# A two-layer graph network on one core: ranking the batch two further on in pieces between VectorE's wide steps

## What is computed

```python
h = jnp.maximum(_layernorm(x, axis=-1), 0.0)
x = x + segment_sum((h * node_vec1)[src], dst, 12500) * node_vec1_n2      # layer 0
h = jnp.maximum(_layernorm(x, axis=-1), 0.0)
x = x + (1.0 + eps[0]) * h + segment_sum(relu(h[src] + edge_attr), dst, 12500)   # layer 1
```

## Time and profile before

| | |
|---|---|
| median of 3 runs | 4801.34 us (4799.08 to 4803.71) |
| the profiled execution, its own time | 4791.23 us |
| span of the profiled execution | 4789.2 us |
| granted TensorE clock, mean | 0.914 |
| layer 0, from one batch's first dst_rel to the next | 113.5 to 122.7 us |

### The profile page before, as it was taken

One profiled execution on the slowest core, in us unless ns is written; L12 is line 12 of the kernel. 1 busy time (PEld: TensorE's weight loads), 2 busy tenths in 40 slices (PEclk: granted clock), 3 DMA queues, 4 the chain that ended last, 5 costly groups with the idle time before them and its releaser, 6 DMA issues.

```text
span 4789.2 us, 130194 instructions
## 1 busy us (share of the span) xinstructions
PE 3721.2 (78%) x43852; PEld 2888.9 (60%) x43852; DVE 3812.7 (80%) x11454; ACT 3261.3 (68%) x9090; POOL 3497.5 (73%) x3590
## 2 busy tenths in 40 slices
PE   0388888888888888888888899467767777777775
PEld 0266666666666666666666666356666666666664
DVE  9788888888888888888888886767777776777775
ACT  1377777777777777777777777456666766666664
POOL 6757777777777777777777777477777777777774
PEclk9999999999999999999999999778888888888887
DMA  6322222222222222222222221211212221211221
GB/s 111 63 51 54 57 54 54 54 56 54 54 54 56 54 53 54 56 54 53 54 56 54 53 54 44 72 39 54 57 43 54 57 57 54 58 49 48 57 57 26
DMA packets 439702, 262.77 MB, mean 55 GB/s; under 512 B 334660, under 2 KB 423732, under 8 KB 432632
## 3 DMA queue, kind: packets, MB, share of 16 engines
q1 hardware_dynamic: 322488, 187.55, 16.7%
q0 software_dynamic: 110816, 60.69, 6.7%
q10 hardware_dynamic: 5728, 5.82, 0.5%
HBM read 172.96 MB, written 80.85 MB: 53 GB/s over the span
## 4 chain that ended last, share of the span: by engine, by line
PE 32%; POOL 23%; DVE 19%; issue 13%; ACT 10%; DMA 2%; DVEq 1%; ACTq 0%; SPq 0%; POOLq 0%
POOL stage L759 22%; PE candidates L1247 18%; PE plain_ps L1259 7%; DVE arena L1753 7%; ACT message L987 5%; DVE arena L1729 4%; ACT centered L956 2%; PE sorted_agg L1187 2%; PE candidates L1157 1%; ACT arena L880 1%; POOL message L759 1%; PE key_rows L1230 1%; DMA stage<-in_edge_attr 1%; DVE counts L1475 1%; PE key_rows L1139 1%
## 5 line engine op out<-in xcount | busy, mean ns | idle before, releaser
L771 POOL DMA_INDIRECT records<-stage,place_i x1875 | 1879.0, 1002 | 696.2 <-issue 652.0
L759 POOL DMA_INDIRECT stage<-table,src_plain x1250 | 1246.9, 997 | 409.1 <-issue 377.3
L987 ACT ACTIVATE message<-candidates,member_is 128x96 bf16<-128x96 f32 x4560 | 1170.7, 377 | 429.4 <-PE candidates L1247 426.3
L1753 DVE TENSOR_SCALAR arena<-window_iota,dst_rel 128x224 bf16<-128x224 f16 (+1 forms) x4800 | 1091.2, 302 | 37.8
L880 ACT ACTIVATE arena<-key_rows 125x640 f16<-125x640 f16 x1000 | 653.2, 716 | 215.1 <-DVE arena L1729 83.2
L1187 PE MATMUL sorted_agg<-arena 128*96 128x224 bf16 (+1 forms) x5000 | 654.1, 285 | 161.0 <-DVE arena L1753 109.6
L1259 PE MATMUL plain_ps<-summed,message 128*96 128x224 bf16 x4560 | 609.2, 269 | 68.2 <-ACT message L987 68.2
L1187 PEld LDWEIGHTS sorted_agg<-arena 128*96 128x96 bf16 x5000 | 543.7, 137 | 186.1 <-issue 118.6
L1259 PEld LDWEIGHTS plain_ps<-summed,message 128*96 128x96 bf16 x4560 | 490.7, 128 | 269.6 <-ACT message L987 127.4
L1729 DVE TENSOR_SCALAR arena<-arena,row_key 125x1280 bf16<-125x1280 f16 x1000 | 554.7, 555 | 96.5 <-ACT arena L880 64.6
L1139 PE MATMUL key_rows<-ident,record 128*125 128x128 f16 x5000 | 425.8, 235 | 239.2 <-DMA record<-records 96.2
(11 more groups left out here) (228 smaller groups left out, 5139.0 us busy)
## 6 DMA issues: line engine op xcount, KB each, us to landing
record<-records SPq DMA_DIRECT2D x50, 1650.0 KB
stage<-in_edge_attr SPq DMA_DIRECT2D x125, 400.0 KB, 3.2
records<-pad SPq DMA_DIRECT2D x25, 1650.0 KB, 11.9
records<-stage,place_i POOLq DMA_INDIRECT x1875
stage<-table,src_plain POOLq DMA_INDIRECT x1250
message<-table,mid_src POOLq DMA_INDIRECT x288
xs<-in_x SPq DMA_DIRECT2D x8, 390.6 KB
table<-parts ACTq DMA_DIRECT2D x4, 585.9 KB
```

The costliest lines, as they stand in the source:

```text
L759: pool.indirect_dma_start(message[:, k, j, :] if l == 0 else rows[:, k, j, :], None, table0 if l == 0 else table1, bass.IndirectOffsetOnAx ...
L771: pool.indirect_dma_start(records, bass.IndirectOffsetOnAxis(ap=place_i[:, h, e:e + 1], axis=0), stage[:, h, e, :], None).then_inc(scatter ...
L987: last = nc.scalar.activation(direct_message[n % DB][:, m * WIDE:(m + 1) * WIDE], candidates[n % 2][:, m * WIDE:(m + 1) * WIDE], ACT.Copy, ...
L1753: last = nc.vector.tensor_scalar(dst_onehot(g, t), window_iota[:, 0:WA if tile == 0 else WT], dst_rel[:, h, tile:tile + 1], None, ALU.is_e ...
```

## The change

`rank_within` is cut in two functions, `rank_buckets` (the small operations and the comparisons) and `rank_scans` (the three scans of one unit). DVE now makes the buckets and the first unit's scans behind wide step 2, the second unit's scans behind wide step 3 and the third's behind wide step 4. `rank_sums` and `rank_places` move from behind the last wide step to behind wide step 6, so that wide step 7 comes after them. PE's `prefixes` move from ahead of wide step 6 to ahead of wide step 5. Operations, shapes and semaphores are the same.

```diff
@@ TensorE, step0
-                            if n == FIRST[SUBS - 2] and left_after(b) >= 2:
+                            if n == FIRST[SUBS - 3] and left_after(b) >= 2:
                                 prefixes(b + 2)
@@ VectorE
             def rank_within(b, h, u):
+                rank_buckets(b, h, u)
+                for v in range(SORTED):
+                    rank_scans(b, v)
+
+            def rank_buckets(b, h, u):
                 nth = [0]
...
-                for v in range(SORTED):
-                    for some in SCANS:
-                        last = nc.vector.tensor_tensor_scan(counts[:, v, some], goes_on[:, 0:some.stop - some.start],
-                                                            in_bucket[:, v, some], 0.0, ALU.mult, ALU.add)
-                        if v < SORTED - 1 or some != SCANS[-1]:
-                            step(last)
-                last.then_inc(scans_ready, 1)
-                assert nth[0] == RANK1
+                assert nth[0] == 8 + SORTED
+
+            def rank_scans(b, v):
+                nth = [8 + SORTED + v * len(SCANS)]
...
+                for some in SCANS:
+                    last = nc.vector.tensor_tensor_scan(counts[:, v, some], goes_on[:, 0:some.stop - some.start],
+                                                        in_bucket[:, v, some], 0.0, ALU.mult, ALU.add)
+                    if v < SORTED - 1 or some != SCANS[-1]:
+                        step(last)
+                if v == SORTED - 1:
+                    last.then_inc(scans_ready, 1)
+                    assert nth[0] == RANK1
@@ VectorE, step0
                             sort_some(b, q, i, s)
                             direct_onehots(b, h, s)
-                            if s == SUBS - 3 and more:
-                                rank_within(b + 2, h, u + 1)
-                        if more:
-                            rank_sums(b + 2)
-                            rank_places(b + 2, h, u + 1)
+                            if s == 2 and more:
+                                rank_buckets(b + 2, h, u + 1)
+                            if s in (2, 3, 4) and more:
+                                rank_scans(b + 2, s - 2)
+                            if s == SUBS - 2 and more:
+                                rank_sums(b + 2)
+                                rank_places(b + 2, h, u + 1)
                         first_onehots(*after(b, h, u))
```

More of the change, by code:

```diff
@@ L1449, in rank_within, with step @@
                         bucket16[:, v * J:(v + 1) * J].unsqueeze(1).to_broadcast([P, BUCKETS, J]), ALU.is_equal))
-                for v in range(SORTED):
-                    for some in SCANS:
-                        last = nc.vector.tensor_tensor_scan(counts[:, v, some], goes_on[:, 0:some.stop - some.start],
-                                                            in_bucket[:, v, some], 0.0, ALU.mult, ALU.add)
-                        if v < SORTED - 1 or some != SCANS[-1]:
-                            step(last)
-                last.then_inc(scans_ready, 1)
-                assert nth[0] == RANK1
+                assert nth[0] == 8 + SORTED
+            def rank_scans(b, v):
+                nth = [8 + SORTED + v * len(SCANS)]
+                def step(ins):
+                    nth[0] += 1
+                    ins.then_inc(rank1_steps, 1)
+                    dve.wait_ge(rank1_steps, b * RANK1 + nth[0])
+                for some in SCANS:
[6 more added lines that the diff above has]
+                    assert nth[0] == RANK1
             HALVINGS = []
```

## The result

The changed kernel takes 4903.79 us (median of 4 runs, 4896.35 to 4915.81) beside 4802.32 us of the kernel before on the same chip (4 runs, 4799.08 to 4803.71): a ratio of 1.0215, 95% interval 1.0192 to 1.0237, or 101 us more. The profiled execution took 4896.35 us, with a span of 4894.3 us and a mean granted clock of 0.910.

What follows compares the result with a forecast made beforehand. Neither DVE (80% busy) nor PE (78%) bounds throughout: PE leads in main groups' waiting, DVE is ahead in wide steps. 4791.2 + 75 (late group 2) + 9 (clock) = 4876, plus 10.1 for the median: 4886 us; range 4836 to 4932.

Steps and rivals of the forecast that it cites:

- Pieces and prefixes: Wide steps 3 to 5: DVE's lead hides the moved work, no PE wait; DVE gets 2.8 us of waits back.
- PE waits about 3.1 us for wide step 7: Sums and places delay wide step 7's first pair to 1235.6 us; PE has wanted it since 1232.47.
- DVE's saved work turns into a wait for ACT's key copies: Step's end: the 14.6 us taken out become DVE waiting, 4 to 6 us for key copies ahead of `first_onehots`.
- Group 2 is 2.6 us late without a loop turn and 4.0 with one: Next batch's group 2 starts late: 12 x 2.6 + 11 x 4.0 = 75 us over 23 ranking steps.
- The clock: a quarter of 38 us: PE behind its new waits: slower clock costs 1.64 us at most in each of 23 steps; 9 us taken.
- the wait of 2.39 us in the earlier trace: A PE wait in the old kernel that cost nothing, used for the clock's lower bound of nothing.
- the 113 us that the prediction worked out for that case: Loss if the clock falls at every new PE wait: 75 + 38 = 113 us instead of 84.
- The clock at each wait: Rival: the clock falls at every new PE wait for wide step 7, 113 us more, 4914 us; chance 0.19.
- Faster: Rival: wide step 7 is in time, group 2 begins 1.75 us earlier at 12 ends, 4780 us; chance 0.07.
- The earlier wide steps: Rival: PE also stands at wide step 3, whose margin is 0.8 us; 23 us more, 4909 us; chance 0.08.
- The scatters: GpSimd's 75 scatters begin earlier, `ranked` coming some 5 us earlier; gains nothing and costs nothing.

Runs made afterwards that it cites:

- without the pieces: Changed kernel with buckets and scans again in one piece behind wide step 5, prefixes ahead of wide step 6, sums and places still ahead of wide step 7: 4992.95 us, 1.0388.
- the kernel that stays busy through the wait: Changed kernel plus twelve matmuls on PE just ahead of wide step 7's first tile, their results written over: 4886.82 us, ratio 1.0166 to the kernel before.
- the pieces alone: Changed kernel with sums and places back behind wide step 7, scans and prefixes still early: 4796.17 us, ratio 0.9975 to the kernel before.
- the sums alone: Changed kernel with only the places moved back behind wide step 7, sums staying ahead of it: 4797.53 us, ratio 0.9979 to the kernel before.
- pieces, sums ahead and earlier keys: Changed kernel with places back behind wide step 7 and key rows of groups 0 and 1 turned and copied one tile earlier: 4774.55 us, ratio 0.9943.
- earlier keys without the sums: Changed kernel with sums and places back behind wide step 7, key rows of groups 0 and 1 one tile earlier: 4784.55 us, ratio 0.9972.

## Why the prediction was right

**Pieces and prefixes cost nothing, and give 2 to 3 us of DVE's time.** Right. In the changed kernel wide step 3 begins at 1237.85 us, 3.9 us before PE's first tile at 1241.78 (predicted lead 3.9); for wide step 5 it is 5.5 us (1255.19 to 1260.70; predicted 4.6). PE has no idle there. The wait ahead of wide step 5 fell from 55.6 to 5.4 us, and without the pieces PE's wait is 6.6 us a step (151.9 over 23) instead of 3.8.

**PE waits about 3.1 us for wide step 7.** Right: 3.39 us in this step, 3.18 at the end with a loop turn, 83.5 us over 22 waits or 3.8 each; the first is 6.7. That this wait carries the loss is shown: with the places behind wide step 7 the wait goes and so does the loss. The count was one too high. The last ranking step has no sorting rounds, DVE reaches its wide step 7 in time there, and the step isn't longer: a test of the mechanism that the kernel makes by itself. It also answers a rival that the experiments leave open, since moving the places back moves the scatters back too: in this step the scatters begin 18.4 us ahead of group 2 instead of 9.1, as early as in the others, and nothing is lost. The other steps grew by 4.7 to 4.8 us on average, the first by 9.2, more than the 3 to 4 that the prediction named.

**DVE's saved work turns into a wait for ACT's key copies.** Right: 5.98 us in this step, and 238.6 us of such waits instead of 64.6.

**Group 2 is 2.6 us late without a loop turn and 4.0 with one: 75 us.** Near in sum, by luck: the two errors cancel. With the clock held at most of the waits for wide step 7 the loss is 1.66% of 4802 us, or 80 us; the changed kernel's further 24 us are the clock. In the trace of the kernel that stays busy through the wait, the ends are 4.0 us longer without a loop turn and 3.1 with one. The first number was too small for two reasons. PE's first tile of wide step 7 is later than the 3.4 us of the prediction: where PE was kept busy it ends 3.9 us later than if it had begun in place of the twelve matmuls (1274.38 + 1.52 against 1270.85 + 1.18), and ACT hands that on to group 1's keys. And the step that was read did not stand for its kind. There DVE began group 2 1.75 us behind its keys, and the prediction let 0.8 of the 3.4 us vanish in DVE's own lateness, at all twelve ends without a loop turn. At ten of these twelve ends of the kernel before, group 2 begins only 0.03 to 0.51 us behind its keys: ACT's copies set its time already, and nearly the whole delay passes on. One of the ten, ACT's copy of group 2's keys, DVE's group 2, and PE's first pick and last products in the timelines of the kernel before:

```profile
1719.75 1.30 ACT L880 ACTIVATE arena<-key_rows 125x640 f16<-125x640 f16 x2
...
1721.17 1.17 DVE L1729 TENSOR_SCALAR arena<-arena,row_key 125x1280 bf16<-125x1280 f16 x2
...
1714.77 1.52 PE L1157 MATMUL candidates<-parts,arena 125*128 125x96 bf16 x20 [2.39 <-ACT message L987]
1716.09 3.26 PE L1259 MATMUL plain_ps<-summed,message 128*96 128x224 bf16 x20
```

Even in the step that was read the slack is used up, by slow last products. ACT's copies for groups 1 and 2 begin 5.94 us apart there; where PE was kept busy through the wait they are 8.55 apart (1282.20 to 1290.75), with last products of 3.94 us between them instead of 2.08. Why the number for the ends with a loop turn was too large is not shown.

**The clock: a quarter of 38 us.** The mis-sized term. The prediction let it fall at few of the waits; it fell at 20 of 22. In each of those 20 steps at least one five-matmul tile behind the wait takes 2.0 to 2.2 us; at the full clock the first takes 1.5, since it follows DVE, and the second 1.18, as behind the two shortest waits (1.61 and 1.64 us). It costs some 24 us (1.0215 - 1.0166 = 0.0049, with an interval of about 0.0027 either way, so 11 to 36 us), more than the 9 taken and less than the 38 of the rival. Both were priced from the wrong tiles: 1.64 us is what the last products lose, and these were slow at most ends already. They took 2.08 us at only 5 of the 24 ends of the kernel before, 2.7 to 3.94 at the others, though PE's wait ahead of the pick was 2.4 us at 19 of them; so the wait of 2.39 us in the earlier trace rows that cost nothing was the exception. On average the last products take 3.2 us before and 3.2 in the changed kernel. What the new falls cost is seen in the tiles of wide step 7 (526.1 us of picks from xs before, 555.1 in the changed kernel, 535.6 where PE was kept busy and the first tile still followed DVE). The Trainium skill (TensorE: Matmul & The Clock Gate, Part 1) says that idling brings the half rate back. The trace agrees in these 20 steps, with a mean granted clock of 0.71 to 0.72 behind a wait of 3.39 us; the 113 us that the prediction worked out for that case were nearer to the 101 measured than the 84 forecast.

**The rivals.** The clock at each wait came nearest (4914 us) but overstates the price. Faster is ruled out for this order; the point that the prediction named for it, DVE earlier by some 3 us at wide step 7, is met when the places, 4.6 us, stay behind: then PE all but doesn't wait and the kernel is 0.2% faster, less than the 21 us (0.44%) of this rival, which took the slack of 1.75 us for all twelve ends. The earlier wide steps were not late. The scatters start earlier against group 2, by 17.7 us instead of 7.2 (1283.58 in the changed kernel, before), and nothing was seen to come of it.

**What stays open.** The profiled execution of the pieces alone (span 4791.9 us) isn't shorter than that of the kernel before (4789.2), though the medians differ by 0.25%. The two come from different occasions: the execution profiled before took 4791.23 us, 11 us below that kernel's median of 4802.32; that of the pieces alone took 4793.97, 2 us below its own. So the two traces can't show where the 0.25% lie.

## What to carry to other kernels

When work is moved ahead of something that another engine needs, measure the producer's lead at that place and compare it with the work's length: here 9.4 us of lead against 14.6 us of work less 2.8 us saved, and the sums alone, 9.9 us, which fitted into the lead with what was saved, cost nothing. Time saved on an engine that is ahead only shows up at its next wait (a room, then the keys, then the next keys), so each must be moved in turn: pieces, sums ahead and earlier keys gave 0.57% together, and earlier keys without the sums nothing that could be measured. Before one step stands for all, look at its kind in the whole trace: the slack of 1.75 us was there at two ends of twelve. Price a new TensorE wait as its length plus the slower tiles behind it.

## What the runs showed of the hardware

Matmuls that compute nothing of use made the kernel faster. Twelve of them in a wait of TensorE, in each of 23 steps, held the granted clock at 1.00 in the step shown, where it otherwise had a mean of 0.71, and the kernel took 0.5% less time with 276 matmuls more. The lower level can begin behind a wait or within it: in the step shown the granted clock still reads 1.00 while PE stands (1280 to 1283 us) and falls once PE works again; in the changed kernel's third wait, of 5.34 us, it reads 0.50 while PE still stands:

```profile
543.70:545.30 1.60, 0.00 (x0) 0.00 (x0) 1.48 (x6) 0.00 (x0) 0.00 (x0) 0.50 1.64 147
```
